# A two-layer transformer block: rope and latent products on rounded high and low parts, and the stage ahead of the 16-wide heads' tiles cut into small pieces

## The chip, the core and the metric

The kernel runs on one core of one Trainium2 chip. TensorE (PE) multiplies matrices, VectorE (DVE), ScalarE (ACT) and GpSimd (POOL) work element by element, and SyncE (SP) issues the DMAs. The metric is the device time of one execution in microseconds (us), the median of several runs. Lower is better.

## The reference, cut to what matters

Two layers on 1024 tokens of width 256. Each is: normalise, attention, add, normalise, mixture of experts, add. Only the first layer's attention is touched. It adds two attentions, weighed by a softmax gate: a main one with 16 heads (rope parts of width 64, latent values of width 64) and a "pattern" one with 16 heads of width 16.

```python
q_mid = rmsnorm(hidden_states @ q_a_w.T, q_a_ln_w)                  # 192 wide
q = (q_mid @ q_b_w.T).reshape(b, s, H, D_Q).transpose(0, 2, 1, 3)   # per head 128 + 64
q_nope, q_pe = (q[..., :D_NOPE], q[..., D_NOPE:])
kv_a = hidden_states @ kv_a_w.T                                     # 64 shared + 16 x 64
k_pe = k_pe_flat.reshape(b, s, H, D_ROPE).transpose(0, 2, 1, 3)
kv = rmsnorm(kv_lora, kv_a_ln_w) @ kv_b_w.T
q_pe, k_pe = apply_rope(q_pe, cos, sin), apply_rope(k_pe, cos, sin)
scores = jnp.einsum('bhqd,bhkd->bhqk', qf, kf) * scale
main_out = softmax(scores) @ v, then @ o_w.T
pattern_out = softmax(pq @ pk.T / 4) @ pv, then @ sp_o_w.T          # 16 heads of 16
return gates[..., 0:1] * main_out + gates[..., 1:2] * pattern_out
```

## The kernel before, in words

Everything is one program with an instruction order per engine that Python lists write out (`pattern_order`, `main_order`, `experts_order` and so on). Every engine walks the same list and runs its own part of each step, in order; semaphores (`wait_ge`, `then_inc`) carry the dependencies. So a PE instruction that waits holds back all that PE has behind it.

**Head.** PE turns the normalised tokens into `hT` (256 x 1024), makes four 128x512 projections of the pattern heads' queries and keys (`pe_project`, blocks 0 and 1, two matmuls each, `project_bank`), four folds of value and output weights (`pe_fold` steps 0 to 11, line 1119), the modulation columns and gates, the token-major rows (`pe_raw`, line 1001) and the values (`pe_value`, line 969). A projection goes to PSUM, ACT stores its rounded high part (`act_project2`, line 868) and DVE the rest (`dve_project2`, line 875, semaphore `pj_low`). SP writes both to a DRAM scratch (`sp_scratch2`, semaphores `so`) and loads them back stacked by head (`sp_stack2`, semaphores `stacked`) into `qstr` and `kstr`.

**The stage ahead of the tiles.** The list `pattern_order` begins with 22 maxima steps. A maximum (`pe_maxp` line 1281, `dve_maxp` line 1289) is two 64-row matmuls over 128 queries and 512 keys for a head pair, into one of two ring slots of PSUM, and a DVE reduction over 1024 columns. Eight maxima make one w; then DVE negates and splits the result (`dve_negp`: lines 1295, 1302, 1304), PE turns it (`pe_shift`, line 1314; the first two go to a ring slot) and ACT puts it into two rows of `qstr`. Beside the maxima, the dictionary `beside` sets other steps: folds 4 to 7 (line 1124, of the query-by-key weights; three list steps of one fold stand together, two of PE and one of ACT), the projections of blocks 2 and 3, and eight turns of the latents (`pe_latents`, lines 1078 to 1080, each of which needs a piece that POOL makes, `pool_latents`). All folds 4 to 7 use bank 7 or 6, as the projections of blocks 2 and 3 use bank 7.

**The tiles.** Then 128 steps s follow, each with two score tiles (`pe_stp`, line 1414), two exponentials (`act_expp`, line 1435, into `Pb` buffers of which the first lie over the projections' staging: tile 0 waits for `so[0]`, tile 4 for `so[1]`, that is for the scratch writes of blocks 2 and 3), two pieces of the product with the values (line 1457), and one maximum until none is left. Beside the steps from s = 64 the first head pair's preparation runs, each product cut in two.

**Preparation of a head pair.** Six products of 128x512 (`pe_part`, line 1536): four rope parts (two of keys from `wkpe` and `hT`, two of queries from `wqpa`, `wqpb` and `qmTa`, `qmTb`) and two latent parts (from `waba`, `wabb`). Each is two float32 matmuls over 128 rows. ACT copies the bank to `t12` (line 1574), SP swaps its halves by DMA, POOL applies the rope and splits the result into high and low parts (lines 1596 to 1622).

**Main heads.** `main_order` has 32 units, four for a head pair: 4 score blocks of six fp32r matmuls (lines 1712 to 1714), a DVE maximum (1721), an exponential (1736), 32 transposes (1745), copies, the product with the latent values (1805) and the output projection (1826). While a pair runs, the next pair's six products stand between the turns, one every five turns (`PREP_EVERY`); seven pairs are prepared here. POOL has nothing else in this stage. It works in order, so a piece put between two products delays the second.

**POOL before the tiles:** `pool_rest`, `pool_mc`, four memsets of 16x4096 (`pool_stack2`, lines 904 and 906), `pool_latents`, `pool_scale` (line 1847, 128x2048 at once; line 1850), four more memsets. SP loads `wkpe`, `wqpa`, `wqpb` (2 MB) between the first two and the last stacked loads.

## Time and profile before

| what | us |
|---|---|
| median of 3 runs (1342.86 to 1344.18) | 1343.31 |
| the profiled execution's own time | 1348.52 |
| its span, first to last instruction | 1346.6 |
| PE busy | 1278.6 (95%) |
| DVE busy | 776.1 (58%) |
| ACT busy | 734.5 (55%) |
| POOL busy | 487.3 (36%) |
| mean granted TensorE clock, as a share of 2.4 GHz | 0.972 |

Times in the rows count from the span's start. The stages: the head to about 47, maxima and folds to 94, tiles to about 298, main heads to about 815, then experts and the second layer. A busy PE in a row is a modelled busy time: matmuls overlap, so the chain of work, which gives each instruction only what it adds, is the better price.

### The profile page before, as it was taken

What the parts mean: (1) busy time and instruction counts of PE and PEld (TensorE: products, weight loads), DVE (VectorE), ACT (ScalarE), POOL (GpSimd) and SP (SyncE); (2) the same over time, 40 slices, a digit from 0 to 9 for tenths busy, and PEclk for the clock granted to TensorE, in tenths of its full rate; (3) what the DMA queues carried; (4) which work ended last, traced back from release to release, by engine and by line L of the source; (5) the groups of instructions that cost most, each with busy time, mean ns of one, the idle gap of its engine ahead of it and who ended that gap; (6) DMA issues with size and microseconds to landing.
All of it is one profiled execution on the core that took longest, in us unless ns stands there. A gap on an engine that the chain in (4) does not pass through costs nothing.

```text
span 1346.6 us, 22054 instructions
## 1 busy us (share of the span) xinstructions
PE 1278.6 (95%) x8233; PEld 873.7 (65%) x8233; DVE 776.1 (58%) x1221; ACT 734.5 (55%) x1364; POOL 487.3 (36%) x439
## 2 busy tenths in 40 slices
PE   7879999999999999999999999999978998889998
PEld 5633443357777777777777777788853444578997
DVE  4478987624545444444444566654767774575555
ACT  3438987775555555555555554333245667435553
POOL 5260045224656657474655303445200000331221
PEclk9969999999999999999999999999999999899999
DMA  8734000001010111111111203001331510101110
GB/s 330 192 75 82 1 10 17 9 1 29 20 33 17 31 25 24 25 24 24 24 24 25 63 13 138 24 25 47 72 81 39 114 36 1 32 15 32 49 40 32
DMA packets 54866, 63.90 MB, mean 47 GB/s; under 512 B 23997, under 2 KB 41149, under 8 KB 53693
## 3 DMA queue, kind: packets, MB, share of 16 engines
q1 hardware_dynamic: 54760, 62.50, 17.4%
q8 instruction: 66, 1.08, 0.4%
q14 instruction: 40, 0.32, 0.1%
HBM read 45.64 MB, written 8.45 MB: 40 GB/s over the span
## 4 chain that ended last, share of the span: by engine, by line
PE 82%; DVE 10%; ACT 3%; issue 2%; DMA 2%; SPq 0%; POOL 0%; ACTq 0%; DVEq 0%; POOLq 0%
PE bank L1805 9%; PE bank L1745 8%; PE bank L1457 7%; PE bank L1536 6%; PE bank L2002 5%; PE bank L2004 5%; PE bank L2003 5%; PE bank L1712 4%; PE bank L1714 4%; PE bank L1713 4%; PE bank L1414 4%; PE bank L1281 2%; PE bank L1826 2%; DVE mpc L1356 2%; PE bank L1394 2%
## 5 line engine op out<-in xcount | busy, mean ns | idle before, releaser
L1721 DVE TENSOR_REDUCE nmq<-bank 128x1 f32<-128x1024 f32 x128 | 156.5, 1223 | 163.8 <-PE bank L1714 163.7
L1435 ACT ACTIVATE Pb<-bank 128x512 f32<-128x512 f32 (+3 forms) x355 | 180.8, 573 | 36.6 <-PE bank L1414 14.1
L1758 ACT ACTIVATE Pt<-bank 128x512 f32<-128x512 f32 x187 | 110.6, 594 | 121.9 <-PE bank L1745 121.0
L1289 DVE TENSOR_REDUCE mp<-bank 128x2 f32<-128x1024 f32 x128 | 154.2, 1223 | 34.0 <-PE bank L1281 33.2
L1736 ACT ACTIVATE Pq<-bank,nmq 128x1024 f32<-128x1024 f32 x127 | 141.7, 1115 | 56.3 <-DVE nmq L1721 56.2
L1745 PE MATMUL bank<-idf,Pq 128*128 128x128 f32 x1016 | 145.8, 275 | 1.4 <-ACT Pq7l L1736 1.2
L1745 PEld LDWEIGHTS bank<-idf,Pq 128*128 128x128 f32 x1016 | 119.2, 140 | 39.3 <-issue 15.6
L1712 PE MATMUL bank<-qk1h,qk0h 128*128 128x512 f32 x256 | 120.6, 471 | 0.0
L1356 DVE TENSOR_REDUCE mpc<-bank 128x2 f32<-128x1024 f32 (+2 forms) x96 | 88.4, 954 | 47.5 <-PE bank L1344 25.2
L1805 PE MATMUL bank<-Pt,kvx 128*64 128x256 f32 x992 | 114.1, 382 | 0.0
L1457 PE MATMUL bank<-Pb,vx 128*17 128x256 f32 (+3 forms) x1222 | 108.9, 416 | 0.7 <-ACT OTa L1471 0.5
L1714 PE MATMUL bank<-qk1h,qk0l 128*128 128x512 f32 x256 | 101.2, 395 | 0.0
L1713 PE MATMUL bank<-qk1l,qk0h 128*128 128x512 f32 x256 | 100.4, 392 | 0.0
L1805 PEld LDWEIGHTS bank<-Pt,kvx 128*64 128x64 f32 x992 | 68.6, 137 | 40.5 <-issue 9.3
L1598 POOL TENSOR_TENSOR t<-t,sinT 128x512 f32<-128x512 f32 x32 | 41.0, 1280 | 107.0 <-DMA t<-t 107.0
L1977 POOL TENSOR_TENSOR cTt<-cTt,gab 128x256 f32<-128x256 f32 x8 | 6.1, 758 | 190.6 <-DVE cTt L1972 190.4
L1414 PE MATMUL bank<-qstr,kstr 64*128 64x512 f32 x256 | 72.1, 507 | 1.0 <-ACT Pb L1435 0.6
L2204 POOL TENSOR_TENSOR hl<-hf,hh 128x512 fp32r<-128x512 f32 x32 | 41.2, 1288 | 84.1 <-ACT hh L2191 84.1
L1596 POOL TENSOR_TENSOR Rt<-t,cosT 128x512 f32<-128x512 f32 x32 | 41.0, 1282 | 72.9 <-ACT t L1574 71.0
L2416 POOL TENSOR_TENSOR v1l<-wr,v1h 128x512 fp32r<-128x512 f32 x25 | 32.1, 1289 | 96.3 <-ACT v1h L2411 96.3
L1414 PEld LDWEIGHTS bank<-qstr,kstr 64*128 64x128 f32 x256 | 28.6, 188 | 58.2 <-ACT Pb L1435 36.4
L1816 DVE TENSOR_TENSOR OTm<-bank,Rs 128x256 f32<-128x256 f32 x32 | 13.6, 424 | 89.4 <-PE bank L1805 87.1
(344 smaller groups left out, 2948.5 us busy)
## 6 DMA issues: line engine op xcount, KB each, us to landing
t<-t SPq DMA_DIRECT2D x128, 64.0 KB
wr<-wf SPq DMA_DIRECT2D x25, 256.0 KB, 2.7
wraw<-wf SPq DMA_DIRECT2D x8, 768.0 KB, 4.3
scratch<-stgr SPq DMA_DIRECT2D x4, 1024.0 KB, 7.8
Rs<-shares SPq DMA_DIRECT2D x64, 64.0 KB, 3.8
scratch<-stg SPq DMA_DIRECT2D x8, 384.0 KB, 2.6
qst<-scratch SPq DMA_DIRECT2D x9, 256.0 KB, 8.6
owT<-owT SPq DMA_DIRECT2D x1, 2048.0 KB, 11.3
```

The source lines that it names most:

```text
L1289: e.tensor_reduce(mp[:, w % 3, :, j, kh], wide[slot][:], AX, ALU.max).then_inc(ring_ok, 1)
L1356: e.tensor_reduce(mpc[:, w // 2 % 3, a0:a0 + 2, j, kh], wide[slot][:, :, 0:c], AX, ALU.max).then_inc(ring_ok, 1)
L1414: e.matmul(bank[b][:], kst2[r, hp, kt * 128:kt * 128 + 128], qst2[r, hp, cols(half)], start=True, stop=True).then_inc(st_mm[0], 1)
L1435: e.activation(PBR[l][i % len(PBR[l])][:, 0:c], bank[b][:, 0:c], ACT.Exp, scale=0.25).then_inc(exp_ok[0], 1)
L1457: last = e.matmul(bank[6][32 * a:32 * a + 17, to:to + c], vx[:, t, h * 17:h * 17 + 17], PBR[l][i % len(PBR[l])][:, q0:q0 + c], start=(t == ...
L1712: e.matmul(o, qh[:, qs], kh[:, ks], start=True, stop=False)
L1713: e.matmul(o, qh[:, qs], kl[:, ks], start=False, stop=False)
L1714: last = e.matmul(o, ql[:, qs], kh[:, ks], start=False, stop=True)
L1721: e.tensor_reduce(nmq[:, n % 8:n % 8 + 1], scores(u, i), AX, ALU.max, negate=True).then_inc(mp_ok, 1)
L1736: e.activation(probabilities(u, i)[:], scores(u, i), ACT.Exp, bias=nmq[:, n % 8:n % 8 + 1], accum_out=sums[:, u % 2, i:i + 1]).then_inc(ex ...
L1745: last = e.transpose(bank[b][:, 128 * c:128 * c + 128], probabilities(u, 2 * (c % 2) + c // 2)[:, 128 * k:128 * k + 128], idf[:])
L1805: last = e.matmul(bank[6][64 * hd:64 * hd + 64, 0:256], kvx[:, k, :], transposed(u, k)[:, 256 * hd:256 * hd + 256], start=(k < 1), stop=(k ...
```

## The change

**Products on parts.** `hT`, `qmTa` and `qmTb` are each rounded once by POOL to a float32r high part and a remainder (`pool_rounded`, 26 instructions). The weights of each product come pair by pair (128 KB loads) and POOL splits them, two instructions each, three splits for a pair (`pool_weights_k`, `_q`, `_l`). A key rope product becomes six fp32r matmuls of 128x512; a query rope product and a latent product become five, since the remaining 64 of the 192 rows are laid twice, as high and low part, over 128 rows. For this two DMAs copy 64 rows below (`sp_below`). The loads of `wkpe`, `wqpa` and `wqpb` and `pool_rest` are gone. New waits: a product waits for `rounded` and for its split (`wt_ok`).

**Small pieces.** In `beside` the two PE steps of each fold and the two matmuls of each projection (`begin`, `project`) stand apart, each behind its own maximum; DVE's remainder (`low`) is a step of its own one or two maxima later. The latents' turns move behind the folds. `fold_bank` spreads the folds over banks 4 to 7, so their waits change. POOL's memsets of the last half are cut into 16 of 16x1024, its scaling of `mo` into 8 of 128x256, and the memsets now run before the scaling. In the head, the first folds wait for one remainder each (`pj_low`, g + 1) instead of all four, the third and fourth of the token-major rows wait for `gate_v` 3 and 7 instead of 8.

```diff
-    beside = {0: folds(4), 1: [("rms", 1), ("project", 2, 0)], 3: folds(5), 4: [("rms", 2), ("project", 2, 1)],
-              6: [("lat", 0), ("lat", 1)], 8: folds(6), 9: [("lat", 2)], 10: [("project", 3, 0)], 11: [("lat", 3)],
-              13: folds(7), 14: [("lat", 4)], 15: [("lat", 5)], 16: [("project", 3, 1)], 18: [("lat", 6)], 19: [("lat", 7)]}
+    beside = {0: [("fold", 12)], 1: [("rms", 1), ("fold", 13), ("fold", 14)], 2: [("begin", 2, 0)], 3: [("project", 2, 0)],
+              4: [("rms", 2), ("fold", 15)], 5: [("low", 2, 0), ("fold", 16), ("fold", 17)],
+              6: [("fold", 18)], 7: [("fold", 19), ("fold", 20)], 8: [("begin", 2, 1)], 9: [("project", 2, 1)],
+              10: [("fold", 21)], 11: [("low", 2, 1), ("fold", 22), ("fold", 23)], 12: [("begin", 3, 0)], 13: [("project", 3, 0)],
+              14: [("lat", 0), ("lat", 1)], 15: [("low", 3, 0), ("lat", 2)], 16: [("lat", 3)], 17: [("begin", 3, 1)],
+              18: [("lat", 4), ("lat", 5)], 19: [("lat", 6), ("project", 3, 1)], 20: [("lat", 7)], 21: [("low", 3, 1)]}
...
     def fold_bank(g):
-        return 6 if g in (1, 3) else 7
+        return (4, 5, 6, 7, 4, 5, 6, 4)[g]
...
-            if g == 0:
+            if g < 4:
                 e.wait_ge(d_w3[0], 32)
-                e.wait_ge(pj_low, 4)
-            elif g in (2, 3):
-                e.wait_ge(fold_ok, g - 1)
+                e.wait_ge(pj_low, g + 1)
...
         if part[0] == "rope" and ROPE[part[1]][0] == 1:
-            two = [(wkpe[:, k, p, :], hT[:, k, cs]) for k in range(2)]
...
+            two = [[(wkh[:, k, :], kmh[:, k, cs]), (wkh[:, k, :], kml[:, k, cs]), (wkl[:, k, :], kmh[:, k, cs])] for k in range(2)]
...
+            two = [[(hi[:, 0, :], qah[:, cs]), (hi[:, 0, :], qal[:, cs]), (lo[:, 0, :], qah[:, cs])],
+                   [(hi[:, 1, :], qbs[:, cs]), (lo[:, 1, :], qbs[:, cs])]]
         for k in ks:
-            last = e.matmul(o, *two[k], start=(k == 0), stop=(k == 1))
+            for n, (w, q) in enumerate(two[k]):
+                last = e.matmul(o, w, q, start=(k == 0 and n == 0), stop=(k == 1 and n == len(two[1]) - 1))
...
+    def pool_weights_q(e, p):
+        e.wait_ge(d_wq, 16 * (p + 1))
+        if p:
+            e.wait_ge(rp_mm, 4 * p)
+        e.tensor_copy(wqh[:], wqs[:]).then_inc(wt_hi, 1)
+        e.wait_ge(wt_hi, SPLIT2["q", p])
+        e.tensor_tensor(wql[:], wqs[:], wqh[:].bitcast(F32), ALU.subtract).then_inc(wt_ok, 1)
+        e.wait_ge(wt_ok, SPLIT2["q", p])
...
-        e.tensor_tensor(mo[:], mo[:], gab[:, 0, :].unsqueeze(1).to_broadcast([128, 8, 256]), ALU.mult).then_inc(sc_ok, 1)
+        for p in range(8):
+            e.tensor_tensor(mo[:, p, :], mo[:, p, :], gab[:, 0, :], ALU.mult).then_inc(sc_ok, 1)
...
     def gpsimd(e):
-        pool_rest(e)
         pool_mc(e, 0)
         pool_stack2(e, slice(0, 4))
         pool_vx_ones(e, 0)
         pool_latents(e)
-        pool_scale(e)
+        e.wait_ge(qkv_ok, NT)
         e.wait_ge(fold_ok, 6)
         pool_stack2(e, slice(4, 8))
+        pool_scale(e)
+        pool_rounded(e)
+        pool_weights_k(e, 0)
+        pool_weights_q(e, 0)
+        pool_weights_l(e, 0)
         for p in range(8):
             if p < 2:
                 pool_keys(e, p)
             for k in range(len(FIRST)):
                 pool_product(e, p, k)
+                if k == 0 and p:
+                    pool_weights_q(e, p)
+                elif k == 3 and p < 7:
+                    pool_weights_k(e, p + 1)
+                elif k == 5 and p < 7:
+                    pool_weights_l(e, p + 1)
...
     def sync(e):
...
-        for d, n in ((wkpe, "wkpe"), (wqpa, "wqpa"), (wqpb, "wqpb")):
-            e.dma_start(d[:], a[n]).then_inc(d_w4, 16)
+        sp_weights_k(e, 0)
+        sp_weights_q(e, 0)
...
+        sp_below(e)
...
         for s in MAIN:
             if s[0] == "prep":
                 sp_swap(e, s[1], s[2])
+                if s[2] == 0:
+                    sp_weights_q(e, s[1])
+                elif s[2] == 2 and s[1] < 7:
+                    sp_weights_k(e, s[1] + 1)
```

## Rows read from the trace of the kernel before

**Rows 1.** Chain of work, whole run, main heads: start, us added, what.
```profile
387.56 3.60 PE bank L1805 x32
...
452.82 3.60 PE bank L1805 x32
...
748.28 3.60 PE bank L1805 x32
...
762.06 3.60 PE bank L1805 x32
```

**Rows 2.** Chain of work from 434 to 452: one product, transposes, score matmuls.
```profile
446.59 1.72 PE bank L1536 x4
448.31 0.87 PE bank L1745 x8
449.18 0.23 PE bank L1712
449.41 0.23 PE bank L1713
```

**Rows 3.** Timeline of POOL: two subtractions of 64x512 in a product.
```profile
458.18 2.63 POOL L1622 TENSOR_TENSOR qk1l<-Rt,qk1h 64x512 fp32r<-64x512 f32 x2
```

**Rows 4.** Waits from 400 to 750: total, times, longest.
```profile
POOL t L1598 <- DMA t<-t: 73.0, 21, 5.7
...
ACT t L1574 <- DMA t<-t: 0.4, 1, 0.4
```

**Rows 5.** Windows: length, busy us (instructions) by engine, granted clock, DMA share, GB/s.
```profile
60.00:85.00 25.00, 20.36 (x78) 11.73 (x78) 17.46 (x16) 5.12 (x9) 8.35 (x12) 0.73 0.10 38
85.00:110.00 25.00, 19.83 (x106) 9.72 (x106) 21.20 (x21) 12.81 (x24) 15.20 (x5) 0.59 0.79 164
110.00:150.00 40.00, 40.00 (x376) 16.64 (x368) 37.60 (x46) 36.30 (x68) 0.00 (x0) 1.00 0.13 31
...
400.00:750.00 350.00, 350.00 (x2101) 252.43 (x2101) 164.79 (x215) 192.04 (x335) 204.72 (x195) 1.00 0.11 25
```

**Rows 6.** Timeline of POOL ahead of the tiles: start, us, line, operation.
```profile
80.45 4.51 POOL L1847 TENSOR_TENSOR mo<-mo,gab 128x2048 f32<-128x2048 f32 x1
84.91 1.26 POOL L1850 TENSOR_TENSOR wsp<-wsp,gab 128x512 f32<-128x512 f32 x1
...
96.92 3.51 POOL L906 MEMSET kstr<- 16x4096 f32 x1
```

**Rows 7.** Timeline of DVE ahead of the tiles.
```profile
53.47 3.48 DVE L1289 TENSOR_REDUCE mp<-bank 128x2 f32<-128x1024 f32 x3
...
62.47 0.17 DVE L1302 CAST mc<-nm 128x8 fp32r<-128x8 f32 x1
...
80.57 4.42 DVE L1302 CAST mc<-nm 128x8 fp32r<-128x8 f32 x1
...
87.26 0.67 DVE L875 TENSOR_TENSOR stgr<-bank,stgr 128x512 fp32r<-128x512 f32 x1
...
98.47 2.00 DVE L1302 CAST mc<-nm 128x8 fp32r<-128x8 f32 x1
```

**Rows 8.** Timeline of PE ahead of the tiles and in the first steps.
```profile
46.85 0.50 PE L1281 MATMUL bank<-kstr,qstr 64*128 64x512 f32 x2
47.49 1.97 PE L1124 MATMUL bank<-kvbk,qbn 128*128 128x64 f32 x16
...
87.48 1.08 PE L1314 MATMUL bank<-idr,mc 128*128 128x128 f32 x4 [5.17 <-DVE mp L1289]
...
94.04 0.80 PE L1414 MATMUL bank<-qstr,kstr 64*128 64x512 f32 x2 [0.45 <-ACT kvT L1087]
...
106.62 0.50 PE L1414 MATMUL bank<-qstr,kstr 64*128 64x512 f32 x2
...
107.84 0.49 PE L1414 MATMUL bank<-qstr,kstr 64*128 64x512 f32 x2
```

**Rows 9.** The scratch writes of the staged projections, issue to landing.
```profile
DMA to landing us min/median/max: 4.0/9.6/12.4
```

More of the change, by code:

```diff
@@ L805, in project_bank, with pe_project @@
         return bank[4 + i if i < 4 else 7]
-    def pe_project(e, blk, half):
+    def pe_project(e, blk, half, ks):
         n, m = BLOCKS[blk]
         i = 2 * blk + half
-        e.wait_ge(hT_ok, 2 * half + 2)
-        if i >= 4:
-            e.wait_ge(fold_ok, i - 1)
-        for k in range(2):
+        if 0 in ks:
+            e.wait_ge(hT_ok, 2 * half + 2)
+            if i == 4:
+                e.wait_ge(v_ok, NT)
+            elif i > 4:
+                e.wait_ge(pj_low, i)
+        for k in ks:
             last = e.matmul(project_bank(i)[:], wsp[:, n, k, m * 128:(m + 1) * 128], hT[:, k, cols(half)],
                             start=(k == 0), stop=(k == 1))
-        last.then_inc(pj_mm, 1)
+        if 1 in ks:
+            last.then_inc(pj_mm, 1)
     def staged_bank(i):
@@ L897, in sp_stack2 @@
                                 rows[:, p0 % 4:p0 % 4 + p1 - p0, :]).then_inc(stacked[g], 16)
+    ONES2 = (4, 20)
     def pool_stack2(e, hps):
-        n = hps.start
+        n, step = (0, 4) if hps.start == 0 else (ONES2[0], 1)
         for par in range(2):
             r = slice(64 * par + 32, 64 * par + 48)
-            e.memset(qst2[r, hps, :].bitcast(F32), 0.0).then_inc(ones2, 1)
-            e.wait_ge(ones2, n + 2 * par + 1)
-            e.memset(kst2[r, hps, :].bitcast(F32), 1.0).then_inc(ones2, 1)
-            e.wait_ge(ones2, n + 2 * par + 2)
+            for st, value in ((qst2, 0.0), (kst2, 1.0)):
+                for h in range(hps.start, hps.stop, step):
+                    e.memset(st[r, h:h + step, :].bitcast(F32), value).then_inc(ones2, 1)
+                    n += 1
+                    e.wait_ge(ones2, n)
     def sp_scratch(e, i):
@@ L1087, in act_latents @@
         e.activation(kvT[:, cs], bank[6][:], ACT.Copy).then_inc(lat_ok, 1)
[L1090 removed]
+    d_wk, d_wq, d_below = sem("d_wk"), sem("d_wq"), sem("d_below")
+    rounded, wt_hi, wt_ok = sem("rounded"), sem("wt_hi"), sem("wt_ok")
+    ROUNDED = 26
+    SPLITS = [("k", 0), ("q", 0), ("lat", 0)]
+    for p_ in range(1, 8):
+        SPLITS += [("k", p_), ("lat", p_), ("q", p_)]
+    SPLIT2 = {s_: n_ + 1 for n_, s_ in enumerate(SPLITS)}
     fold_mm, fold_ok, fold_v = sem("fold_mm"), sem("fold_ok"), sem("fold_v")
     def fold_rows(g):
[L1095 removed]
+        return (128, wab[:, 0, :, :], 8 * (g // 2), 0) if g % 2 == 0 else (64, wab[:, 1, :, :], 8 * (g // 2), 128)
     def fold_bank(g):
[L1098 removed]
+        return (4, 5, 6, 7, 4, 5, 6, 4)[g]
     def pe_fold(e, step):
```

164 lines of the change are left out of this document (120 added, 44 removed).

## The prediction, made before the changed kernel was run

> **What bounds the kernel now.** I read the chain of work first, then the windows by stage, then the timelines of single engines where the chain leaves PE. In the main heads the chain is PE alone. Four units with six products take 452.82 - 387.56 = 65.26 us, a unit without products takes 762.06 - 748.28 = 13.78 [rows 1]. So six products add 65.26 - 4 x 13.78 = 10.14, or 1.69 each; the chain itself gives 1.72 for one [rows 2]. A microsecond taken from PE's products is a microsecond off the end here, as long as nothing else becomes late. In the tiles PE also sets the pace: from 110 to 150 PE is busy all 40 us, but DVE for 37.6 and ACT for 36.3 [rows 5], so the cover over these two is thin. Ahead of the tiles nothing is full. From 60 to 110 the granted clock averages 0.73 and then 0.59 [rows 5], that is, TensorE is at 1.2 GHz for about 54% and 82% of the time. The reader is to see three causes: a fold or a projection is a long piece of PE during which DVE runs out of maxima; DVE's cast of 8 columns takes 4.42 and 2.00 us instead of 0.17 and ends each time with POOL's instruction (the scaling of 2048 columns ends at 84.96, the memset at 100.43) [rows 6, 7]; and PE idles for 5.17 us behind it [rows 8].
>
> **The products on parts.** A product is four passes now, 1.72 us, and the like fp32r matmul of the scores adds 0.23 each time, 0.231 as a mean over six [rows 2]. The new key product is 6 x 0.231 = 1.39, the others are 5 x 0.231 = 1.16. With 1.71 for the old one (between 1.69 and 1.72) a key product saves 0.32 and the others 0.55. Seven pairs are prepared in the main heads: 14 x 0.32 + 28 x 0.55 = 4.5 + 15.4 = 19.9. The first pair, beside the tiles, gives 2 x 0.32 + 4 x 0.55 = 2.8 where PE sets the pace.
> The price per matmul is between the 0.215 that 1.72 / 8 gives for a bare 512-column pass and 0.25, if the change of operands costs as the first matmul behind another kind might; that is 4 us more or 5 less over the 256 matmuls. I take 0.231, since 768 matmuls of the scores have this very shape.
> The Trainium skill ("TensorE: Matmul & The Clock Gate", section on 56 ns against 53.3 ns) gives 215.7 ns from one warm 512-column matmul to the next. By that figure the products would save 256 x 0.015 = 3.9 us more, an estimate from that page; the chain's 0.23 speaks against it.
>
> **What the products cost elsewhere.** POOL gets three splits for a pair, each one cast and one subtraction of 256 columns. A subtraction of 512 columns takes 1.31 [rows 3]; with half of that for each of the two, a split is at most 1.3, and three are 3.9. POOL is busy 204.7 of 350 us and waits 73.0 for the swap DMAs [rows 4, 5], so per pair of 65.3 us it is taken for 38.2 + 13.6 = 51.8. With the splits it is 55.7, and a pair will last 65.3 - 2 x 0.32 - 4 x 0.55 = 62.5. It fits with 7 us to spare. What is queued behind a split on POOL is the next product. The q split stands ahead of product 1, which may then start about a microsecond late. ACT's next copy into `t12` waits for POOL's first multiplication and for the swap DMA; today ACT waits for that only once, 0.4 us [rows 4]. Products now come 0.3 to 0.5 us closer together, so this wait may come up in each pair: between 0 and 7 x 0.7 = 5 us, and I take 0.6, near the row. PE's new waits for a split are covered: a split is made one or two products, 10 to 20 us, ahead of its use. SP's small weight loads stand behind swaps whose products they need, so they hold up nothing that is urgent. The 26 rounding instructions (about 19 us at 0.65 for each 256 columns) and the first splits run while POOL idles today, from 100.4 on; before s = 64 (64 steps after 94 at 1.22) they are long done, even if the two copying DMAs land behind the stacked loads, cosT and sinT. They cost DVE: while POOL is busy a cast of DVE waits for it, now for at most one piece (a quarter of 3.51, 0.88). Four w's may be hit, 0.4 to 1.2 us each; DVE has 2.4 us free in 40 [rows 5], 0.6 in the ten of a w. I take 1.5 us in all (0 to 4), counted in the stage below. Sum of this half: 19.9 + 2.8 - 0.6 = 22.1, with ends 17 and 25.
>
> **The head.** The folds start 1.5 us sooner, since they no longer wait for the last remainder, and 0.8 us goes at the gates. But the first maximum needs the stacked loads, whose DMAs are issued as before. It starts at 46.85, right behind the values [rows 8], so the landing is at or before that. The gain is between 0 and 2.3; SP's queue and the full DMA engines make me take 0.2, and PE idles for 2 us instead. That idle time may cost clock.
>
> **The stage ahead of the tiles.** I walk the new list by hand from 46.7, with the rows' durations at full clock. DVE: 22 maxima at (3.48 - 1.23) / 2 = 1.13 [rows 7] are 24.9, four remainders at 0.6 are 2.4, two splits of maxima at 0.5 and the small gate steps 0.7. That is 29. PE: 22 maxima at about 0.24 (two matmuls in different row groups, side by side), two whole and two half-height folds, at most 1.97 each [rows 8], so 7.9, four projections at 1.72 = 6.9, 24 transposes at 0.11 = 2.6 [rows 2], two shifts 1.2. That is 24. Each slot between two maxima now holds at most 1 us of PE, less than DVE's 1.13. DVE still runs dry in three places: the first two shifts take a ring slot and wait until it is free (0.8 and 0.3 us), and `begin` of block 3 waits for the remainder two steps before (0.3). The walk ends with the last maximum at 78.3, its remainder at 79.1 and the first tile at 78.0 instead of 94.04 [rows 8]: 16 us. PE would then be 76% busy.
> Clock: from 60 to 110 it is at 1.2 GHz for two thirds of the time [rows 5]. I take one third of the new stage at 1.2 GHz, since the 5 us hole behind POOL's scaling is gone but PE idles 2 us at the start. In 10 us PE then falls 5 us behind, of which DVE-bound slots hide 1: first tile at 82.
> Then a wait that before hid: tile 4's exponential needs the scratch write of block 3. Today the remainder is done at 87.93 and the write lands 4.0 later at the soonest [rows 7, 9], ahead of 94. In the new order the remainder is the last step, one microsecond behind the first tile: 83.1 + 0.4 + 4.0 = 87.5 for an exponential that could run at 84.8. That costs 2.7. Six steps more at 1.22 [rows 8] from the third on: the seventh step, which starts at 106.62 today, comes at 87.5 + 4 x 1.22 = 92.4, plus 1.5 for clock, plus the 1.5 for DVE behind POOL's pieces: 95.4. Gain 11.2. Ends: at 1.2 GHz throughout PE needs 48 us for this stage and the gain is about 0; at full clock all the way the seventh step comes at 88.2 + 1 = 89.2, a gain of 17.4.
> The Trainium skill ("SBUF — State Buffer", section "SBUF: two separate sides") says that DVE in a two-port mode and a GpSimd instruction lock each other out for a whole instruction, and that a DVE instruction with two SBUF inputs is held up only by one that reads SBUF. The row agrees for the cast (4.42 until the scaling ends). By that rule memset pieces would stop the cast but not the subtraction behind it; the sum would change by well under a microsecond.
>
> **Sum.** 22.1 + 11.2 + 0.2 = 33.5. The profiled execution took 1348.52 with a span of 1346.6, 1.9 around it and 5.2 above the median; I expect a span of 1313 and, against the median, 1343.3 - 33.5 = 1309.8, rounded to 1310.
>
> **The rivals.**
> **A.** The clock stays low ahead of the tiles. For it: the idle 2 us at the start, and that from 60 to 110 PE was busy for 40.2 of 50 us and the clock was nevertheless at 0.73 and 0.59 [rows 5]. Against it: POOL's long instructions are gone. The stage gives 0 to 4 instead of 11: 1319.
> **B.** Full clock. DVE sets the pace all the way and the tiles start at 78: 17.4 + 22.1 + 0.2, so 1303.5.
> **C.** POOL or the swap DMAs set the pace in the main heads: ACT waits for `t12` in each product, half of the 19.9 is lost. For it: POOL is taken for 51.8 of 65.3 already, and the swap's landing is less than a microsecond ahead of its use in one place per pair. Against it: 7 us are spare. 1320.
> **D.** Slower: the mixed matmuls cost as much as a pass at 1.2 GHz or a full float32 pass pair, 0.43 (1.72 / 4), wherever fp32r follows transposes and other weights. The products then take 256 x 0.43 = 110 instead of 48 x 1.71 = 82, and with 11 gained ahead of the tiles the kernel is 17 slower: 1360. It decides from (82 + 11) / 256 = 0.364 per matmul on. Every score row at 0.23 is against it.
> **E.** The change does not do what it says: what leaves PE's products comes back as waits for splits, and the stage ahead of the tiles keeps its length: 1343.
>
> **How the numbers follow.** Forecast 0.56 (1304 to 1316), A 0.16, B 0.13, C 0.09, D 0.03, E 0.03. The range from 1301 to 1323 holds the forecast, B's middle, A and C, and leaves out what lies beyond the ends. 0.2% is 2.7 us, about what a measurement of this kernel can tell from no change. Faster: all but D and E and a little of C, 0.95. Within 0.2%: 0.02. Slower: 0.03.
>
> **What would show it.** In the profile after: line 1536's successor with 256 matmuls and a pitch of 0.23; units of the main heads that average 15.6 instead of 16.3, still 13.78 without products; ACT's copy into `t12` waiting under 1 us per pair; no DVE cast above 0.9 us ahead of the tiles; first tile near 82, the fifth exponential behind it waiting for the scratch write; the seventh step near 95. The prediction is wrong if the clock row ahead of the tiles reads 0.6 or 1.0 throughout, or if the units without products get longer.

## The result, and the profile after

| | before | after |
|---|---|---|
| median, us (runs) | 1343.74 (1342.86 to 1344.27) | 1319.89 (1316.92 to 1323.4) |
| profiled execution's own time, us | 1348.52 | 1317.4 |
| its span, us | 1346.6 | 1315.5 |
| mean granted TensorE clock | 0.972 | 0.981 |
| PE, DVE, ACT, POOL busy, us | 1278.6, 776.1, 734.5, 487.3 | 1245.6, 772.1, 731.8, 532.5 |

The ratio is 0.9827, with a 95% interval of 0.9808 to 0.9845: 24 us faster, and inside the forecast range, but 10 us above the forecast itself. On the chip of the later runs the changed kernel was 1320.01 against 1345.28, ratio 0.9816 (0.9794 to 0.9838). So 25 to 30% of the forecast gain of 33.5 did not come, and the experiments look for it. Ratios and their intervals go by the mean times of the fast runs alone, so one slow run each of after_three (1325.7) and after_buffers_turned (1334.2) is in the medians below but not in the ratios.

Lines of after are not those of before. Line 1281 (maximum on PE) is now 1312, 1289 (on DVE) 1320, 1302 and 1304 (cast and subtraction of a w) 1333 and 1335, 1414 (tile) 1445, 1435 (exponential) 1466, 1536 (product) 1580, 1584 (swap) 1623, 1598 and 1622 (POOL) 1637 and 1661, 1781 and 1792 (write and read of the shares) 1892 and 1903, 1805 (values) 1916.

The windows of after, in the columns of [rows 5]:

```profile
60.00:85.00 25.00, 20.14 (x89) 10.28 (x87) 19.13 (x21) 8.85 (x17) 11.57 (x19) 0.86 0.16 64
85.00:110.00 25.00, 22.10 (x196) 8.42 (x199) 21.88 (x23) 19.80 (x37) 24.34 (x34) 0.93 0.95 200
110.00:150.00 40.00, 37.52 (x326) 15.52 (x320) 35.05 (x43) 31.01 (x58) 11.33 (x19) 0.91 0.04 8
...
400.00:750.00 350.00, 347.25 (x2232) 270.26 (x2232) 173.91 (x226) 197.16 (x345) 219.76 (x221) 1.00 0.14 34
```

From 60 to 110 the clock is far better than before. But from 110 to 150, where it was 1.00 and PE was busy all 40 us, it is 0.91 and PE lacks 2.5 us. And in the main heads PE, busy for 350 of 350 before, lacks 2.75.

PE ahead of the tiles and in the first steps (its timeline; answers to [rows 8]):

```profile
44.17 0.49 PE L1312 MATMUL bank<-kstr,qstr 64*128 64x512 f32 x2 [0.41 <-issue]
...
81.97 0.51 PE L1445 MATMUL bank<-qstr,kstr 64*128 64x512 f32 x2 [1.30 <-ACT kvT L1108]
...
87.50 0.50 PE L1445 MATMUL bank<-qstr,kstr 64*128 64x512 f32 x1 [2.41 <-ACT Pb L1466]
...
93.20 0.50 PE L1445 MATMUL bank<-qstr,kstr 64*128 64x512 f32 x2
...
113.14 0.66 PE L1345 MATMUL bank<-idr,mc 128*128 128x128 f32 x4 [2.00 <-DVE mc L1335]
```

The first maximum starts at 44.17 instead of 46.85, the first tile at 81.97 instead of 94.04, the seventh step at 93.20 instead of 106.62. Then PE waits 2.00 us for a DVE subtraction. Why, the timelines of DVE and POOL show:

```profile
69.13 0.35 DVE L1333 CAST mc<-nm 128x8 fp32r<-128x8 f32 x1
...
110.21 2.67 DVE L1333 CAST mc<-nm 128x8 fp32r<-128x8 f32 x1
112.91 0.17 DVE L1335 TENSOR_TENSOR mc<-nm,mc 128x8 fp32r<-128x8 f32 x1
```
```profile
108.94 1.17 POOL L1685 CAST qah<-qmTa 128x512 fp32r<-128x512 f32 x2
110.07 2.78 POOL L1689 TENSOR_TENSOR qal<-qmTa,qah 128x256 fp32r<-128x256 f32 x4
```

The cast begins inside a row of four rounding subtractions and ends, at 112.88, when all four have ended, not after the one of 0.70 that was running. Behind PE's idle 2.00 us the clock is at 1.2 GHz from 115.9 to 122.7.

Eleven microseconds earlier the same pair of engines behaves otherwise. POOL's eight multiplications of `mo` stand as close together as the subtractions, one each 0.70 us, and a cast that falls among them ends with the one that is running:

```profile
94.16 5.59 POOL L1959 TENSOR_TENSOR mo<-mo,gab 128x256 f32<-128x256 f32 x8
```
```profile
99.10 0.69 DVE L1333 CAST mc<-nm 128x8 fp32r<-128x8 f32 x1
```

The main heads: first the chain of work of one pair, then the waits from 300 to 770 (engine, line, what it waited for: total, times, longest).

```profile
564.99 3.60 PE bank L1916 x32
...
569.17 1.16 PE bank L1580 x5
...
609.01 1.38 PE bank L1580 x6
```
```profile
POOL t L1637 <- DMA t<-t: 98.0, 25, 12.1
...
ACT t L1613 <- DMA t<-t: 10.8, 3, 4.8
ACT t L1613 <- POOL Rt L1635: 5.2, 2, 2.6
```

A product adds 1.38 or 1.16 to the chain where it added 1.72 [rows 2], and the pair that starts at 564.99 is over at 627.25, after 62.26 us (65.26 before [rows 1]). But the longest wait for a swap DMA has gone from 5.7 to 12.1 (their total, 98.3 before and 98.0 after from 300 to 770, has not moved), and ACT waits for `t12` for 16 us where it waited 2.2 in the same stretch (0.4 from 400 to 750, [rows 4]). The chain from 418 to 446 runs through such a place:

```profile
432.14 0.64 SPq L1903
...
435.40 9.02 DMA t<-t
444.50 1.28 POOL t L1637
```

SP's own timeline says what stood around the late swap:

```profile
423.86 0.40 SPq L1892 DMA_DIRECT2D shares<-rcp  x1
432.14 1.30 SPq L1903 DMA_DIRECT2D Rs<-shares  x2
433.53 2.46 SPq L1623 DMA_DIRECT2D t<-t  x4
436.80 0.37 SPq L1892 DMA_DIRECT2D shares<-rcp  x1
```

SP first waits 8.27 us for the write of the shares (512 pieces of 4 bytes) to land before it may read them back, with the swap queued behind. Here that costs only half a microsecond: ACT's copy that the swap needs ended at 433.01, and the swap was issued from 433.53 on. What is late is its landing. Of its 64 completion events 63 are in by 437.42, and the last comes at 444.43, beside those of the next write of shares (issued at 436.80). The other late swap of this trace, issued up to 498.40, has 62 by 501.39 and the last at 509.47. SP's queue itself holds a swap up in the first pair, where one is issued at 312.51, 5.0 us after it was ready (4.3 in before).

### The profile page after: what moved, and what is told of

It reads as the page before. It is cut to its first block, busy times and chain, and to the rows that moved or that the text cites. A ratio compares the mean times of both kernels' runs of the same rounds, so it can differ in the third digit from the quotient of the medians.

```text
span 1315.5 us, 22364 instructions
## 1 busy us (share of the span) xinstructions
PE 1245.6 (95%) x8297; PEld 876.4 (67%) x8297; DVE 772.1 (59%) x1221; ACT 731.8 (56%) x1364; POOL 532.5 (40%) x531
## 4 chain that ended last, share of the span: by engine, by line
PE 74%; DVE 11%; DMA 5%; POOL 3%; issue 3%; ACT 3%; SPq 1%; ACTq 0%; POOLq 0%; DVEq 0%
PE bank L1916 7%; PE bank L1488 7%; PE bank L1856 7%; PE bank L2114 6%; PE bank L2115 6%; PE bank L2116 5%; PE bank L1580 4%; PE bank L1823 4%; PE bank L1445 4%; PE bank L1825 4%; PE bank L1824 4%; DVE mp L1320 3%; PE bank L1312 2%; DVE mpc L1387 2%; PE bank L1425 2%
## 5 line engine op out<-in xcount | busy, mean ns | idle before, releaser
L1387 DVE TENSOR_REDUCE mpc<-bank 128x2 f32<-128x1024 f32 (+2 forms) x96 | 88.4, 954 | 47.6 <-PE bank L1375 25.2
L1823 PE MATMUL bank<-qk1h,qk0h 128*128 128x512 f32 x256 | 109.2, 427 | 0.0
L1445 PEld LDWEIGHTS bank<-qstr,kstr 64*128 64x128 f32 x256 | 28.0, 186 | 62.9 <-ACT Pb L1466 38.5
## 6 DMA issues: line engine op xcount, KB each, us to landing
owT<-owT SPq DMA_DIRECT2D x1, 2048.0 KB, 11.2
```

Source lines behind the costliest of these rows:

```text
L1387: e.tensor_reduce(mpc[:, w // 2 % 3, a0:a0 + 2, j, kh], wide[slot][:, :, 0:c], AX, ALU.max).then_inc(ring_ok, 1)
L1445: e.matmul(bank[b][:], kst2[r, hp, kt * 128:kt * 128 + 128], qst2[r, hp, cols(half)], start=True, stop=True).then_inc(st_mm[0], 1)
L1823: e.matmul(o, qh[:, qs], kh[:, ks], start=True, stop=False)
```

## The experiments

All runs are set against the kernel before on the same chip. In the table, the columns are read from each profiled execution: the start of the first maximum (its weight load), and from each mark to the next: the first tile's exponential, POOL's first cast of rotated keys (the product of s = 64, 10.6 us behind that step's tiles; called s = 64 below), the first values product of the main heads, the first matmul of the experts, the end of the span.

| kernel | first maximum | to first tile | to s = 64 | to first values | main heads | to the end | median, us |
|---|---|---|---|---|---|---|---|
| before | 46.9 | 47.9 | 102.7 | 124.7 | 493.5 | 530.9 | 1343.7 |
| before_again | 46.8 | 46.3 | 103.1 | 124.8 | 493.2 | 533.1 | 1349.2 (one run) |
| before_rows | 47.1 | 46.4 | 101.7 | 124.7 | 493.8 | 525.9 | 1342.6 |
| after | 44.1 | 38.4 | 107.3 | 121.6 | 477.6 | 526.5 | 1319.9 |
| after_again | 45.1 | 39.7 | 103.5 | 121.6 | 479.7 | 529.2 | 1320.0 |
| pieces_alone | 47.4 | 41.3 | 101.8 | 124.7 | 493.5 | 530.3 | 1338.2 |
| products_alone | 46.1 | 48.0 | 103.1 | 121.6 | 480.4 | 535.1 | 1333.4 |
| after_own_waits | 44.6 | 37.3 | 103.8 | 121.5 | 478.8 | 529.8 | 1323.2 |
| after_shares_rows | 45.8 | 38.5 | 108.0 | 121.6 | 473.2 | 529.9 | 1316.7 |
| after_rows_kept | 44.6 | 39.8 | 103.4 | 121.5 | 473.7 | 529.4 | 1317.1 |
| after_buffers_turned | 44.9 | 36.9 | 107.5 | 121.6 | 477.5 | 528.4 | 1322.3 |
| after_rows_own | 44.6 | 40.0 | 102.2 | 121.5 | 473.6 | 528.4 | 1313.7 |
| after_three | 46.1 | 38.8 | 102.0 | 121.5 | 473.6 | 530.7 | 1314.8 |
| after_three_filled | 47.2 | 37.1 | 101.0 | 121.5 | 473.7 | 528.3 | 1313.1 |

Single executions of one kernel scatter by up to 16 us on these chips (after_own_waits: 1317.7 to 1333.9), so the medians tell differences of some 3 us at best; the columns repeat much better. The last one, 526 to 535, is work that the change does not touch, and scatters most.

### Each half alone

pieces_alone has the new `beside`, the memsets and scaling in pieces and the waits that go with them, but the old products. products_alone has the old list ahead of the tiles and the new products. The edits below are set against after.

```diff
 pieces_alone
-            two = [[(wkh[:, k, :], kmh[:, k, cs]), (wkh[:, k, :], kml[:, k, cs]), (wkl[:, k, :], kmh[:, k, cs])] for k in range(2)]
+            two = [(wkpe[:, k, p, :], hT[:, k, cs]) for k in range(2)]
 products_alone
-    beside = {0: [("fold", 12)], 1: [("rms", 1), ("fold", 13), ("fold", 14)], 2: [("begin", 2, 0)], 3: [("project", 2, 0)],
+    beside = {0: folds(4), 1: [("rms", 1), ("project", 2, 0)], 3: folds(5), 4: [("rms", 2), ("project", 2, 1)],
```

> The kernel before with the small pieces only (order of the stage ahead of the tiles, fold banks, head waits, POOL's memsets and scaling in pieces); products stay float32. Theory 1: in the changed kernel this part won 13.4 us by the seventh tile step and 5.7 of it were lost again before step 64, because a DVE cast stood behind POOL's rounding and the clock fell. Without rounding the 13.4 stay: 1330 to 1331. Rival: the 5.7 go to DVE being the pace whenever the tiles start early, rounding or not: 1336. The first maximum should start near 44.2 in both.

> The changed kernel with the order, the banks, the waits and POOL's long instructions of before ahead of the tiles; only the products on parts remain. Theory 1: 16 to 20 us from the main heads, 2.5 from the first pair, and the cast behind the rounding costs up to 4 of it again: 1321 to 1326. Rival (the two parts only work together, since the rounding needs POOL early): above 1328. Units of the main heads average 15.6, first tile at 94 less the head's 2.7.

Measured: 1338.16, ratio 0.9955 (0.9933 to 0.9978), and 1333.39, ratio 0.9917 (0.9890 to 0.9943). Both missed their forecasts on the side of the rivals. For the products the table says where: the main heads take 480.4, 13 less than before instead of 20, with a late swap on the chain as in after:

```profile
434.04 8.77 DMA shares<-rcp
446.09 11.20 DMA t<-t
```

and its last stage is 5.8 us longer than the mean of the others (529.3), which nothing in the edit explains. Its rival named the right time, but nothing in the trace shows the reason that it gave: the first product comes at 187.03, as before (187.29), and no cast behind the rounding takes over 0.4. For the pieces the chain of work shows it at the very start:

```profile
43.76 3.64 issue
47.40 0.79 PE bank L1290 x2
48.19 1.90 PE bank L1133 x8
```

PE idles 3.64 us ahead of the first maximum, since SP could issue the stacked loads only at 36.90 (33.97 in after), when the scratch writes had landed. Behind this hole the clock is at 1.2 GHz for 10 us: a fold step takes 1.90 instead of 1.03. So the pieces gain 6.6 us between first maximum and first tile where after gains 9.5 with the same list. (In this kernel line 1290 is the maximum and 1133 the fold.) In every trace but that of the last kernel, which has a filler, the first maximum comes 9.9 to 10.9 us behind the issue of the first stacked load, and in all of them that issue waits 8.8 to 11.5 us for a scratch write.

Theory 1 is half right for the pieces. From the seventh step (99.5 here) to the mark of s = 64 they take 91.0 us, where before takes 90.8 and after 96.6: without the rounding nothing is lost there, so the rival's reason is out though its time is nearer. What is missing is missing ahead of the seventh step, 7.1 us gained instead of 13.4.

### A wait on the own end behind each rounding subtraction

```diff
             e.tensor_tensor(qal[:, ts], qmTa[:, ts], qah[:, ts].bitcast(F32), ALU.subtract).then_inc(rounded, 1)
+            e.wait_ge(rounded, 14 + q + 1)
```

The same stands behind the subtractions into `kml` and `qbs`: 16 waits.

> The changed kernel with one more wait behind each of the 16 subtractions of the rounding, for that subtraction's own end. Theory 2: DVE's cast of 8 columns took 2.67 us because POOL ran four subtractions back to back without a gap; with a gap behind each, no cast ahead of step 64 is longer than 0.9, PE does not idle 2 us there, the clock stays up, and the kernel gains 3 to 6: 1314 to 1317. Rival: DVE waits as long as POOL has anything to do, gap or not: casts of 2 to 3 us stay and the time is 1320.

Measured: 1323.15, ratio 0.9859 (0.9827 to 0.9890); the profiled execution took 1317.7. The median does not confirm the gain. The traces do, for the stage. Here POOL's row of four takes 3.16 instead of 2.78. The cast ends just as the row begins, and the subtraction behind it, which falls into the row, waits for one piece only:

```profile
111.13 3.16 POOL L1690 TENSOR_TENSOR qal<-qmTa,qah 128x256 fp32r<-128x256 f32 x4
```
```profile
110.97 0.23 DVE L1333 CAST mc<-nm 128x8 fp32r<-128x8 f32 x1
111.23 0.67 DVE L1335 TENSOR_TENSOR mc<-nm,mc 128x8 fp32r<-128x8 f32 x1
```

The fairest pair is a cast that begins while the last of the eight key subtractions runs, in after_buffers_turned (without the waits) and in after_three (with them):

```profile
108.74 4.06 DVE L1333 CAST mc<-nm 128x8 fp32r<-128x8 f32 x1
```
```profile
112.61 0.33 DVE L1333 CAST mc<-nm 128x8 fp32r<-128x8 f32 x1
```

The first waits through that subtraction, two casts and four more subtractions, to 112.80; the second gets in behind the one that runs.

The kernels with both halves, taken together, show more. Without these waits the cast near 110 took 2.67, 2.67 and 4.06 us (after, after_shares_rows, after_buffers_turned), and each time the clock fell behind it and "to s = 64" reads 107.3 to 108.0. In two traces (after_again, after_rows_kept) it came at 114.22 and 113.66, in a hole of POOL, took 0.17, and the column reads 103.5 and 103.4:

```profile
114.22 0.17 DVE L1333 CAST mc<-nm 128x8 fp32r<-128x8 f32 x1
```
```profile
117.87 1.17 POOL L1692 CAST qbh<-qmTb 128x512 fp32r<-128x512 f32 x2 [4.03 <-DMA wab<-wab]
```

(POOL had ended its subtractions at 113.83 and waited 4.03 us for a DMA.) With the waits, in after_own_waits, after_three and after_rows_own, no cast behind 95 us is over 0.8 us (one at 88, beside POOL's other pieces, took 1.04) and the column reads 102.0 to 103.8. Counted from the seventh step, where the clock of the first tiles no longer blurs it, the way to s = 64 is 96.6 to 97.6 us with the long cast and 90.8 to 91.8 in the eleven traces without it, those of before among them. So the loss is real, some 6 us, but it hits only the executions in which the cast falls into that row. What the waits change is shown; why this row held DVE out when the multiplications and the key casts, just as close together, let it in after one piece (0.35 to 0.70 us in after, after_again, after_shares_rows, after_rows_kept and after_buffers_turned) is not.

### The write of the shares in 16-byte pieces

after_shares_rows writes each partition's four shares as they lie, so each query's weights go to a wrong query: the output is not the reference's. after_rows_kept does it rightly: the reads bring 2044 bytes to each partition and DVE takes every second element. Since a row of them fills the space of two units, there is one buffer where there were two, and a read also waits until the unit before has been multiplied.

```diff
 after_rows_kept
-        e.dma_start(shares[u % 2].rearrange("j a p -> p (j a)"), rcp4[:, u % 2, 0:4],
-                    allow_slow_non_contiguous=True).then_inc(d_shares, 16)
+        e.dma_start(shares[u % 2].rearrange("(p k) -> p k", k=4), rcp4[:, u % 2, 0:4]).then_inc(d_shares, 16)
...
-            e.dma_start(Rs[64 * hd:64 * hd + 64, u % 2, :].rearrange("c (j p) -> c j p", j=2),
-                        shares[u % 2, :, hd, :].partition_broadcast(64)).then_inc(d_spread, 16)
+            e.dma_start(Rs[64 * hd:64 * hd + 64, 0:511],
+                        shares[u % 2, hd:hd + 511].partition_broadcast(64)).then_inc(d_spread, 16)
```

> The changed kernel, but the write of the reciprocals of the main heads' sums to DRAM goes as 128 rows of 16 bytes instead of 512 elements of 4 bytes; the reads are unchanged, so the weights of queries are permuted (that part of the computation is changed). Theory 3: a swap DMA issued within about a microsecond of that write gets its last landing only with the write's, 8 us on; two of seven pairs were hit in the profile, about 4 us in all, and how many are hit differs from run to run. With a write that lands in 2 to 4 us no swap makes POOL wait over 6 us, the main heads are 3 to 5 us shorter, and the runs lie within 2 us: 1315 to 1317. Rival: the swaps are late because of the new weight loads on the same queue: two long waits of 9 to 12 us stay, 1320.

> The changed kernel itself, once more, as the measure for the other runs on the same chip. Theory 3 (the swap transfers of the main heads are late because they queue behind the write of the shares): 1317 to 1323, and again two to four places in the main heads where a swap lands 9 to 12 us after its issue, so that the first values product and the last matmul of the main heads lie 476 to 481 us apart (before: 493.5). The rival (the late swaps of the first profile were an accident of that execution): no such place, 473 to 474 us, and a median near 1315.

> The write of the shares goes out as 128 pieces of 16 bytes instead of 512 of 4 bytes, and the two reads bring 2044 bytes to each partition, from which VectorE takes every second element; nothing of the computation is changed. Theory 3: the swaps are no longer on the chain, the main heads take 473 to 474 us from the first values product to their last matmul, as in the run with permuted weights (473.2), and the time is 4 to 5 us below that of the changed kernel on this chip, 1315 to 1317. Rival: the permuted run was only lucky, or the larger reads (256 KB instead of 128 KB) cost what the write gives back: within 2 us of the changed kernel.

Measured: after_shares_rows 1316.74, ratio 0.9811 (0.9785 to 0.9836); after_again 1320.01, ratio 0.9816 (0.9794 to 0.9838); after_rows_kept 1317.09, ratio 0.9798 (0.9773 to 0.9822). The medians came as theory 3 had them, but the runs of after_shares_rows lie 11 us apart and not 2. after_again has the late swap once more, with 94.1 us of POOL's waiting and 12.1 as the longest, and 479.7 us of main heads; but it is one swap (issued up to 434.98, landed at 446.37) and not two to four. The rest of its 6 us goes in the first pair, which takes 64.5 us where an undisturbed one takes 62.3, with SP at the read of the shares while swaps are ready. Behind the late swap PE idles 2.3 us and the clock is at 1.2 GHz for 3.4 us from 447.6, so that pair takes 66.4. In the kernels with larger pieces no DMA is on the chain between 290 and 800 us, and the main heads take 473.2 and 473.7: that the small pieces of this write cost 4 to 6 us there is shown, since after_shares_rows changes nothing else of the timing. From 300 to 770, the waits of SP and of POOL in after_rows_kept:

```profile
SPq L1902 <- DMA shares<-rcp: 3.6, 3, 1.7
```
```profile
POOL t L1637 <- DMA t<-t: 63.9, 27, 3.8
```
The wait of SP for the same write in after:

```profile
SPq L1903 <- DMA shares<-rcp: 150.7, 24, 9.9
```

SP stood 150.7 of 470 us for the write in after, and 3.6 with the larger pieces. But it stood 140.2 us for it in before too, where that cost nothing, so the total of such waits is not the price. The medians give 3 us of the 4 to 6, within their scatter.

> The kernel before with the write of the shares in 16-byte pieces; nothing of the computation is changed. In the profile of the kernel before, the swaps are never late for the end, although it writes the same 512 pieces of 4 bytes. Theory 3 as it stands (the write hurts only where swap and write come together on the queue and TensorE has no slack left): within 1 us of the kernel before, and 493 to 494 us from the first values product to the last matmul of the main heads. Rival (the write costs the main heads of the kernel before as well, unseen): 3 us or more below it.

The same edit in the kernel before: 1342.59 against 1344.52, ratio 1.0005 (0.9983 to 1.0026; two of the twelve runs took 1353, which moves the mean and not the median), main heads 493.8. So the write cost nothing before, though it was there, and it became a cost only with the new products.

What makes a swap meet it badly stays open. A write of shares is issued within 2 us behind a swap's last DMA 13 or 14 times in each trace with that write, before's as well as after's. In before, before_again and pieces_alone no such swap lands over 4 us after its issue. In the five traces that have the new products and the write in 4-byte pieces six do, 9.0 to 11.6 us after it, and the others land as before (1.9 to 3.7).

### The probabilities' buffers turned

```diff
-    Pbp = Pb[:9] + [sb(f"Pb{i}", [128, 512], F32, at=HTP + 12 * 1024 + 2048 * (i - 12)) for i in (12, 13)]
+    Pbp = [Pb[8]] + [sb(f"Pb{i}", [128, 512], F32, at=HTP + 12 * 1024 + 2048 * (i - 12)) for i in (12, 13)] + Pb[:8]
```

The waits for `so[0]` and `so[1]` move from tiles 0 and 4 to tiles 3 and 7.

> The eleven buffers of the first tiles' probabilities are handed out in another order, so that tiles 3 and 7 instead of 0 and 4 of block 3's staging space wait for the scratch writes, a step or more later. Theory 4 (the exponential behind the scratch write costs the 2.4 us that TensorE idles ahead of it): the idle 2.4 us are gone, the seventh step starts 2 us sooner and the time falls by 2 us. Rival: the clock and the wait for VectorE set this stretch anyway, so nothing is gained, within 1 us of the changed kernel.

Measured: 1322.31, ratio 0.9819 (0.9786 to 0.9852). The idle 2.41 us behind the exponential is gone, but a cast and the clock took its place: from the first tile to the seventh step it is 10.4 us instead of 11.2 (81.32 to 91.73, after 81.97 to 93.20). The rival is right: under 1 us of the 2.4.

### Combinations

> All three edits in one kernel: own-end waits behind the rounding subtractions, the shares in 16-byte pieces, the probabilities' buffers turned. If the three losses are what the profile says and independent (4 + 4 + 2 us), 1309 to 1312, which is the forecast of 1310. If the stage ahead of the tiles loses to the clock what it gains in waits, 1314 to 1317.

> The changed kernel with the shares in 16-byte pieces and the waits on the own end behind the rounding subtractions, without the turned buffers. Theory 2 (the casts of the tiles wait for a whole row of GpSimd instructions without gaps, and what TensorE idles behind one of them brings the clock down for 6 us): no cast over 0.9 us, no stretch at 1.2 GHz behind 110 us, and 1313 to 1316, as with all three edits (1314.8). Rival: the turned buffers carry the gain of that run, and this one stays at the 1317 of the shares alone.

Measured: after_three 1314.77, ratio 0.9752 (0.9723 to 0.9782); after_rows_own 1313.68, ratio 0.9794 (0.9763 to 0.9826). By the medians both are 5 to 6 us below the changed kernel; after_three's interval lies wholly below that of after_again, that of after_rows_own does not. after_three missed the 1309 to 1312 that independent losses would have given and lies where its other case put it; after_rows_own came as expected. From the start to the experts they take 782.0 and 781.9 us (after 789.0, before 815.7). The turned buffers add nothing to the other two. Between 110 and 790 us neither has a stretch at 1.2 GHz. after_rows_own has one from 46.5 to 53.3, behind a hole of 1.12 us ahead of the first maximum, and its 40.0 us to the first tile are the most of all kernels with the pieces but pieces_alone.

### The kernel before once more

> A second look at the kernel before, for the terms of the sum that were read from one execution. If that execution was typical: the first tile at 94, s = 64 at 197, the main heads 493.5 and 530 us behind them. If its 5 us above the median were in one stage, this look shows which.

Measured: 1349.21, span 1347.3. It has the first tile at 92.3 instead of 94.0, s = 64 at 196.2 instead of 197.5, main heads of 493.2, and 533.1 us behind them, 2 us more than the first trace and 7 more than before_rows. So what lay above the median in both is mostly in the last stage, which scatters.

### The hole ahead of the first maximum filled

```diff
+        if (w, j, kh) == (0, 0, 0):
+            for i in range(8):
+                e.matmul(wide[0][:, 0, 0:256], hT[:, i % 2, 0:128], WQKV[0][:, 2, i % 2, :], start=True, stop=True)
         if (j, kh) == (0, 0):
             e.wait_ge(stacked[min(hp // 2, 2)], STACKED2)
```

> All three edits, and eight matmuls of 128x256 into the first maxima's bank, whose results are overwritten, between the values and TensorE's wait for the stacked loads: 1.7 us of work in the hole that was 0.4 to 3.6 us long in the profiles so far. Theory 5 (the idle hole ahead of the first maximum brings the clock to 1.2 GHz for the next 6 to 10 us, which costs up to 4 us): no stretch at 1.2 GHz between 45 and 60 us, first maximum to first tile 37 to 38.5 us even where the stacked loads land late, and 1312 to 1315. Rival: the clock falls in the holes between the first maxima anyway, which wait for VectorE; then this kernel takes what the one with the three edits takes, or a microsecond more where the loads are early: 1315 to 1317.

Measured: 1313.06, ratio 0.9789 (0.9761 to 0.9817). The chains of after_three and of this kernel, from the end of the values on:

```profile
43.86 2.26 issue
46.12 0.49 PE bank L1312 x2
46.62 1.03 PE bank L1155 x8
...
48.08 1.79 PE bank L1155 x8
...
50.59 2.00 PE bank L831 x2
```
```profile
43.85 3.45 PE bank L1308 x16
47.31 0.43 PE bank L1315 x2
47.74 1.03 PE bank L1155 x8
...
49.21 1.03 PE bank L1155 x8
...
50.67 1.06 PE bank L831 x2
```

With the hole, the second fold step takes 1.79 and a projection 2.00: the clock is at 0.54 and 0.50 from 48 to 54. With the hole filled it is at full speed until 75, and first maximum to first tile takes 37.1 instead of 38.8. So the hole brings the clock down here, and theory 5 holds in this pair of traces. Its length alone does not decide: 1.21 us in after_again were followed by full speed until 72.2, 1.12 us in after_rows_own by 1.2 GHz. But the filler took 3.45 us, twice what was meant, since each of these float32 matmuls goes out as two, and held the first maximum back by about a microsecond. The medians, 1313.1 and 1314.8, don't tell the two apart.

## Why the prediction was right in its parts and 10 us off in its sum

**Products in the main heads: right.** 1.38 and 1.16 per product were forecast as 1.39 and 1.16. The forecast of 19.9 for all is met to the tenth of a microsecond wherever swaps are not late: 493.5 - 473.6. The nearest row decided well; by the Trainium skill's figure of 215.7 ns ("TensorE: Matmul & The Clock Gate", section on 56 ns against 53.3 ns) it would have been 3.9 us more, and the chain of after has 0.23 for each. Rival D (0.43 per matmul) is out. The first pair gave 3.1 (124.7 to 121.6) where 2.8 was forecast.

**ACT behind `t12`: the step that failed.** The forecast took 0.6 us out of 0 to 5, near the one row of 0.4, and named 7 us of POOL time as spare. POOL was indeed not the bound. But the swap DMA was, and its landing was priced as in the rows, 5.7 us at most. Beside the small pieces of the shares it took 9.0 to 11.6 us in one or two places of a trace, and in the first pair SP stood at the read of the shares while swaps were ready. Cost: 5.0 us (478.6 on the mean of the two traces, against 473.6), most of it in one pair each, 65.1 and 66.4 us instead of 62.3. This is rival C's mechanism, the swap DMAs' half of it, with about half of the 10 us that it was given. Its warning, "the swap's landing is less than a microsecond ahead of its use in one place per pair", was the row to price.

**The head: wrong in the reason, not by much.** 0.2 was forecast, with the landing of the stacked loads as the bound. The bound is right, but what moves it is when the scratch writes land, which SP waits for 8.8 to 11.5 us, so the first maximum comes at 44.1 to 47.4 in kernels with the same list (without the filler). Three traces of the old head give 46.8 to 47.1.

**The stage ahead of the tiles: near in place, by luck.** The first tile was forecast at 82 and came at 81.97, but from a first maximum 2.5 us earlier; the stage itself took 37.8 and not 35.3, and in after_again, the same kernel, the tile came at 84.35. A maximum costs PE 0.43 in this stage (44.17 to 44.59) and not 0.24. The Trainium skill ("TensorEngine Tiling (Array Packing)", section "Key Properties") says that different tiles can run matmuls in parallel. The records agree that far: the two matmuls of a maximum start 3 ns apart (45.626 and 45.629). But behind a fold or a projection the pair adds 0.43 to the chain, and 0.23 only where another such pair stands right ahead of it, in the tiles; why is not shown. The clock was taken at 1.2 GHz for a third of the stage; it was there for 6.8 us before the first tile and 3.4 behind it (10.2 and 10.2 around it in after_again). The wait for the scratch write came as forecast: 2.41 idle against 2.7; the row that its 4.0 us were read from [rows 9] counts the loads back too, but 4.0 is also the least of the four writes alone. The seventh step came at 93.20 and, in after_again, at 97.49; forecast 95.4.

**DVE behind POOL's pieces: the second step that failed.** "At most one piece, 0.88" was the assumption. It held, or nearly, behind the memsets, the multiplications and the key casts (0.21 to 1.04), but a cast can wait through the whole row of `qmTa` subtractions, 2.67 or 4.06 us. What PE idles then is followed by 1.2 GHz for 7 to 10 us. In after this gave back 5.8 of the 13.4 us that the seventh step had gained; in after_again it did not happen. The Trainium skill ("SBUF — State Buffer", section "SBUF: two separate sides") has the lock for one whole instruction; here it outlasted three more. The smaller half of that rule, as the prediction worked it out, came true: behind the memset pieces the casts took 0.75 to 1.04 us in eight traces (0.21 in after) and the subtractions of the same w 0.17, behind the multiplications both took 0.65 or more in after (99.10 to 100.47). Why waits on the own end let DVE in was not separated from the mere delay of 0.1 us.

**The rounding's place.** "64 steps after 94 at 1.22" puts step 64 at 172; it came at 186.8 in before, since a step took 1.45 on the mean. The conclusion, that the rounding is done by then, held all the same: the last first split ends at 123.3 in after.

**The reference point.** The sum was made against one execution. Second and third traces of the old list have s = 64 at 196.2 and 195.2 instead of 197.5, so about 1.2 us of the gain had never been there. To the start of the experts the mean of three traces before is 814.5 and of two after 789.3: 25.2 gained, which is the difference of the medians (25.3 on that chip). The 31 us between the two profiled executions are these and the scatter of the last stage.

The missing 8.3 of 33.5 are thus: 4.2 in the main heads and the first pair (17.9 gained, forecast 22.1), by the late swaps, and 4.1 between the start and s = 64 (7.3 gained, forecast 11.4), of which 2.9 on the mean of the two traces for the long cast and its clock, and 1.2 for the reference point. With the shares in larger pieces and the own waits, 32.6 of the 33.5 are there by the start of the experts (814.5 - 781.9); the medians say 31. That this is so near the forecast is partly luck, since the head gained 2.3 us instead of 0.2 and the stage behind it took longer than forecast.

**Not settled.** Why single executions of one kernel scatter by 10 to 16 us when the columns up to the experts repeat within a few; why one row of GpSimd subtractions held a cast out when other rows did not; why the write of 4-byte pieces holds up the last landing of some swaps issued just before it and not of most; why the two halves give 17 us by their medians where the whole gives 24; and why the scratch write takes 9 us in some executions and 11 in others.

## What to carry to other kernels

When the bound engine gets faster, a transfer that always landed in time can become the bound: look for those whose landing is less than a microsecond ahead of their use, and price them by what stands on their queue. Here a write in 4-byte pieces was free at one pace and cost 5 us at the next. Cutting a long GpSimd instruction into pieces frees VectorE in most places, but not in all of them; see in the trace that each wait ends with a piece, and try a wait between the pieces where it doesn't. And a sum made against one profiled execution needs a second trace of the same kernel before its last few microseconds mean anything.

## What the runs showed of the hardware that was not expected

- A DVE cast of 8 columns waited 2.67 us through four GpSimd subtractions of 0.70 each, issued back to back (two traces), and 4.06 us through those and the three instructions ahead of them. Among multiplications and key casts just as close together it waited for about one (0.35 to 0.80 in eight traces). With a gap of about 0.1 us behind each subtraction it took at most 0.8 behind 95 us.
- A write of 2 KB from 128 partitions as 512 pieces of 4 bytes landed 7.8 to 9.1 us after its issue where the chain shows it; as 128 pieces of 16 bytes the median from issue to landing is 1.4 to 1.6. The Trainium skill ("DMA: Bandwidth & Descriptors", section "Specifications") says that transfers below 512 B are read, modified and written; both of these are below that, so by it alone they would be alike.
- A swap of 128 partitions of 2 KB by four DMAs had 63 of its 64 completion events within 2.0 us of the last issue and the last one 7.0 us later, when a write in 4-byte pieces had been issued 1.4 us behind it.
- A hole of 2.3 us in TensorE was followed by 1.2 GHz 2.1 us later and for 6.8 us; matmuls of no use in its place kept 2.4 GHz for 28 us more. Holes of 1.12 and 1.21 us in two other kernels differed: the first was followed by 1.2 GHz, the second was not.
